# Index tiles turned by transposing transfers instead of TensorE, and the low parts of the looked-up weights and of the paired stage's h made on GpSimd

## The reference

```python
# attention, on the normalised x; scores are 512 x 512 per batch
q, k, v = x @ Wq, x @ Wk, x @ Wv
attn_scores = jnp.einsum('bes,bfs->bef', qT, kT) / np.sqrt(HEAD_DIM)
attn_weights = jax.nn.softmax(attn_scores, axis=-1)
attn_output = jnp.einsum('bef,bfs->bes', attn_weights, vT)
return jnp.einsum('bse,ef->bsf', jnp.swapaxes(attn_output, 1, 2), Wo)
...
# feed-forward network: w = lut[idx], three index matrices of 1376 x 512 int32 (down is 512 x 1376)
gate = _ghost_linear(x, gate_idx, lut)
up = _ghost_linear(x, up_idx, lut)
h = jax.nn.silu(gate) * up
return _ghost_linear(h, down_idx, lut)
...
x = x + attn(layernorm(x)); x = x + ffn(layernorm(x))
```

## Time and profile before

| | |
|---|---|
| Median of 3 runs | 1046.42 us (1044.93 to 1046.98) |
| The profiled execution's own time | 1046.57 us |
| Its span, first to last instruction | 1044.6 us |
| PE busy | 1010.1 us, 97% of the span |
| DVE, ACT, POOL busy | 485.5, 465.3, 134.5 us |
| DVE busy in the 40 slices of 26 us | 5 to 9 tenths up to slice 15, then 0 to 4 |

### The profile page before, as it was taken

One profiled execution on the slowest core, in us unless ns is written; L12 is line 12 of the kernel. 1 busy time (PEld: TensorE's weight loads), 2 busy tenths in 40 slices (PEclk: granted clock), 3 DMA queues, 4 the chain that ended last, 5 costly groups with the idle time before them and its releaser, 6 DMA issues.

```text
span 1044.6 us, 12958 instructions
## 1 busy us (share of the span) xinstructions
PE 1010.1 (97%) x4744; PEld 833.8 (80%) x4744; DVE 485.5 (46%) x1019; ACT 465.3 (45%) x753; POOL 134.5 (13%) x136
## 2 busy tenths in 40 slices
PE   5979999999999999999999999999999999999998
PEld 4878877878788868888888887888888888888886
DVE  5897998989999942311131113111311131112001
ACT  5999998797899921221222122212221222122111
POOL 5410000000000000110111011101110111011111
PEclk9999999999999999999999999999999999999999
DMA  9963012031011182200220002002200020001001
GB/s 239 200 170 103 21 54 89 6 129 46 29 71 49 66 317 86 101 1 1 81 81 1 1 1 82 1 1 81 81 1 1 1 81 1 1 1 41 1 1 40
DMA packets 31756, 61.42 MB, mean 59 GB/s; under 512 B 8704, under 2 KB 19152, under 8 KB 27344
## 3 DMA queue, kind: packets, MB, share of 16 engines
q1 hardware_dynamic: 18432, 54.40, 14.2%
q0 software_dynamic: 8944, 4.24, 3.5%
q10 hardware_dynamic: 4320, 1.97, 0.7%
HBM read 43.98 MB, written 20.84 MB: 62 GB/s over the span
## 4 chain that ended last, share of the span: by engine, by line
PE 80%; DVE 9%; ACT 5%; issue 3%; DMA 1%; POOL 1%; ACTq 0%; POOLq 0%; SPq 0%; DVEq 0%
PE bank L1018 44%; PE bank L1026 21%; PE bank L960 10%; DVE part L1208 2%; PE bank L1061 2%; DVE bn L1185 1%; PE bank L974 1%; DVE picked L1208 1%; PE bank L1007 1%; ACT part L753 1%; ACT xg_n L854 1%; ACT idx_out L846 1%; DVE xg_lo L1227 1%; DMA xg<-in_L_attn_x 1%; POOL rstd L717 1%
## 5 line engine op out<-in xcount | busy, mean ns | idle before, releaser
L1018 PE MATMUL bank<-x2t_hi,w_hi 128*128 128x512 f32 (+1 forms) x704 | 275.2, 391 | 3.8 <-DVE x2t_lo L1305 3.5
L1018 PE MATMUL bank<-x2t_hi,w_lo 128*128 128x512 f32 (+1 forms) x704 | 274.8, 390 | 0.0
L1018 PE MATMUL bank<-x2t_lo,w_hi 128*128 128x512 f32 (+1 forms) x704 | 274.7, 390 | 0.0
L1432 DVE TENSOR_TENSOR h_full<-bank,h_gate 128x512 f32<-128x512 f32 (+1 forms) x66 | 45.6, 691 | 396.5 <-PE bank L1018 396.5
L753 ACT ACTIVATE part<-high_bit,lut,lut_step 128x512 f32<-128x512 uint8 x198 | 154.5, 812 | 14.2 <-DVE part L1208 8.6
L1018 PEld LDWEIGHTS bank<-x2t_hi,w_hi 128*128 128x128 f32 (+1 forms) x704 | 130.8, 186 | 34.0 <-issue 4.7
L1018 PEld LDWEIGHTS bank<-x2t_lo,w_hi 128*128 128x128 f32 (+1 forms) x704 | 130.9, 186 | 29.6
L1018 PEld LDWEIGHTS bank<-x2t_hi,w_lo 128*128 128x128 f32 (+1 forms) x704 | 130.8, 186 | 29.2
L933 ACT ACTIVATE h_gate<-bank 128x512 f32<-128x512 f32 (+1 forms) x66 | 39.5, 598 | 256.5 <-PE bank L1018 256.5
L712 POOL TENSOR_TENSOR h_lo<-h_full,h_hi 128x512 fp32r<-128x512 f32 (+1 forms) x66 | 85.3, 1292 | 507.9 <-ACT h_hi L936 507.9
L1026 PE MATMUL bank<-w_hi,h_hi 128*128 128x512 f32 (+1 forms) x324 | 129.6, 400 | 0.1
(11 more groups left out here) (151 smaller groups left out, 1329.9 us busy)
## 6 DMA issues: line engine op xcount, KB each, us to landing
xg<-in_L_attn_x SPq DMA_DIRECT2D x7, 1024.0 KB, 6.8
x1a<-in_L_attn_x SPq DMA_DIRECT2D x4, 1024.0 KB, 4.9
out_dram<-x1a SPq DMA_DIRECT2D x4, 1024.0 KB, 3.9
x1b<-in_L_attn_x SPq DMA_DIRECT2D x3, 1024.0 KB, 4.9
m_hi<-m_scratch SPq DMA_DIRECT2D x3, 1024.0 KB, 4.8
m_lo<-m_scratch SPq DMA_DIRECT2D x3, 1024.0 KB, 6.9
out_dram<-x1b SPq DMA_DIRECT2D x3, 1024.0 KB, 3.9
h_scratch<-h_kept_hi SPq DMA_DIRECT2D x10, 256.0 KB, 2.0
```

The lines of the kernel that those rows point to most:

```text
L1018: last = pe.matmul(tile[0:n, :], a, x, start=(k == 0 and j == 0), stop=(k == K - 1 and j == 2))
L1432: dve.tensor_tensor(h_full[0:n, :], bank[5][0:n, :], h_gate[0:n, :], ALU.mult).then_inc(h_done, 1)
```

## The change

- PE's transposes of the index tiles, their PSUM copies on ACT and SP's stores of them are gone. In their place POOL's queue first casts the indices to uint16 from DRAM to DRAM (`narrow`, 19 transfers in six parts), SP issues 33 transposing transfers from there into eight SBUF buffers `idx_wide` (`turn_idx`), and POOL's queue stores each of these as bytes (`store_idx`).
- `narrow_at`, `turn_at` and `store_at` give the places: place i is Gram item i up to 31, and for entry `n` of the product stage it is n + 28. Turns 0 to 11 stand at places 9 to 30, turns 12 to 32 at places 31 to 51, one each; every store stands two places behind its turn.
- `weight_low` of all 33 tiles and `h_low` of the 22 pairs move from DVE to POOL (`weights_low`, with a table of its own, `POOL_LOOKS`).
- x of the Gram stage has four buffers instead of three (`idx_bf` is gone), so loads run a group further ahead.
- The tables are new. Their digits add up to this before the first product (`n` = 8): DVE 48 of 429 steps before, 21 of 396 now; ACT 33 of 294 before, 15 of 294 now; POOL 2 of 33 now. A tile has 13 steps on DVE before and 12 now.

```diff
+    NARROW = [slice(0, 1), slice(1, 2), slice(2, 4), slice(4, 6), slice(6, 8), slice(8, C)]
...
-        xg = [at(f"xg{i}", kib, [P, T, D], F32) for i, kib in enumerate((76, 84, 156))]
+        xg = [at(f"xg{i}", kib, [P, T, D], F32) for i, kib in enumerate((76, 84, 156, 92))]
...
-        idx_bf = [at(f"idx_bf{i}", 92 + 1 * i, [P, D], BF16) for i in range(16)]
-        idx_out = [at(f"idx_out{i}", 176 + i / 2, [P, D], U8) for i in range(4)]
+        idx_wide = [at(f"idx_wide{i}", 172 + i, [P, D], U16) for i in range(8)]
...
+        narrow_at = [2, 10, 16, 24, 30, 34]
+        turn_at = [9, 10, 11, 16, 18, 20, 22, 24, 26, 28, 29, 30] + list(range(31, 52))
+        store_at = [place + 2 for place in turn_at]
...
-            "0040000620100004200000062000004500010000600010009020000020202001007001008030000000902000801000601000"
-            "000000500000a04000d020060500402000d020080300702000c020060400602000c020080200802000c020070200401"
...
+            "0040050050000250000003300000053000004100010000800100007000000030003001008000009000300100823000700000"
+            "600002000000400000c00000e0000a0000700000c0000a0000900000d000090000800000g000070000800000e000080000e"
...
         @blk.sync
         def _(sp):
-            def store_idx(u):
-                if u < STRAIGHT:
-                    return
-                sp.wait_ge(idx_laid, u + 1)
-                sp.dma_start(idx_dram[u], idx_out[u % 4][:]).then_inc(idx_stored[u % 4], 16)
+            def turn_idx(u):
+
+                c, kind, slot = u // 3, u % 3, u % len(idx_wide)
+                if kind == 0:
+                    for part_, run in enumerate(NARROW):
+                        if run.start == c:
+                            sp.wait_ge(idx_narrowed[part_], 16 * (4 if run.stop == C else 3))
+                if u >= len(idx_wide):
+                    sp.wait_ge(idx_stored[slot], times_stored(u - len(idx_wide)))
+                n = rows(c)
+                if kind < 2:
+                    src = (gate_dram, up_dram)[kind][c * P:c * P + n, :]
+                    dst = idx_wide[slot][:].rearrange("p (k o) -> p k o", k=K)[:, :, 0:n]
+                else:
+                    src, dst = down_dram[:, c * P:(c + 1) * P], idx_wide[slot][:]
+                sp.dma_start(dst, src, transpose=True).then_inc(idx_turned[slot], 16)
...
-                if g >= 3:
-                    sp.wait_ge(xg_normed, T * (g - 2))
-                sp.dma_start(xg[g % 3][:], xb_dram[g]).then_inc(xg_loaded[g % 3], 16)
+                if g >= 4:
+                    sp.wait_ge(xg_normed, T * (g - 3))
+                sp.dma_start(xg[g % 4][:], xb_dram[g]).then_inc(xg_loaded[g % 4], 16)
...
+            def narrow(part_):
+
+                run, done = NARROW[part_], idx_narrowed[part_]
+                span = slice(run.start * P, min(run.stop * P, I))
+                for src, dst in ((gate_in, gate_dram), (up_in, up_dram)):
+                    pool.dma_start(dst[span, :], src[span, :]).then_inc(done, 16)
+                pool.dma_start(down_dram[:, span], down_in[:, span]).then_inc(done, 16)
+                if run.stop == C:
+                    pool.dma_start(down_dram[:, I:C * P], down_in[:, 0:C * P - I]).then_inc(done, 16)
+
+            def store_idx(u):
+
+                slot = u % len(idx_wide)
+                pool.wait_ge(idx_turned[slot], times_stored(u))
+                dst = idx_in[u][:] if u < STRAIGHT else idx_dram[u]
+                pool.dma_start(dst, idx_wide[slot][:]).then_inc(idx_stored[slot], 16)
...
-            for stage, arg in timeline:
-                if stage == "idx_load":
-                    load_idx(arg)
+            def weights_low():
+
+                for u in range(U):
+                    c, kind = u // 3, u % 3
+                    pool.wait_ge(w_hi_done, u + 1)
+                    low(w_lo[c][:, kind, :], picked[u % 2][:], w_hi[c][:, kind, :]).then_inc(w_lo_done, 1)
+                    yield
+
+            for stage, arg in with_looks(POOL_LOOKS, weights_low()):
+                if stage == "narrow":
+                    narrow(arg)
+                if stage == "idx":
+                    store_idx(arg)
...
+                if stage == "h_low":
+                    b, c = arg
+                    n, q = rows(c), pair_count[arg]
+                    hi, lo = h_kept if b else (h_hi[c % 2], h_lo[c % 2])
+                    pool.wait_ge(h_hi_done, q)
+                    low(lo[0:n, :], h_full[0:n, :], hi[0:n, :]).then_inc(h_lo_done, 1)
```

More of the change, by code:

```diff
@@ L162, in preln_attention_ghost_ffn @@
         xg_first_loaded = [sem(f"xg_first_loaded{t}") for t in range(T)]
-        xg_loaded = [sem(f"xg_loaded{i}") for i in range(3)]
+        xg_loaded = [sem(f"xg_loaded{i}") for i in range(len(xg))]
         xg_stats = sem("xg_stats")
@@ L315, in preln_attention_ghost_ffn @@
         timeline += [("gram_low", 0), ("stats_shift", 1), ("gram_n", 1), ("gram_in", 1), ("gram_n", 2), ("lut_step", 0)]
-        timeline += [("idx_load", u) for u in range(IDX_AHEAD)]
-        u = 0
         for i in range(T * NG):
@@ L333, in preln_attention_ghost_ffn @@
                 timeline.append(("gram_in", i + AHEAD))
[L334 to L336 removed]
+            index_steps(i)
             timeline.append(("gram", i))
@@ L684, in _ @@
             pool.memset(ident[:], 0.0).then_inc(const_made, 1)
-            pool.memset(ident_bf[:], 0.0).then_inc(const_made, 1)
-            for tile in idx_out:
-                pool.memset(tile[:], 0).then_inc(idx_cleared, 1)
-            pool.wait_ge(const_made, 2)
-            for one in (ident, ident_bf):
-                pool.affine_select(out=one[:], in_=one[:], compare_op=ALU.not_equal, fill=1.0, base=0,
-                                   pattern=[[-1, P]], channel_multiplier=1).then_inc(const_made, 1)
+            pool.wait_ge(const_made, 1)
@@ L1418, in _ @@
                     dve.tensor_tensor(h_full[0:n, :], pair_bank(arg)[1][0:n, :], h_gate[0:n, :], ALU.mult).then_inc(h_done, 1)
-                if stage == "h_low":
-                    b, c = arg
-                    n, q = rows(c), pair_count[arg]
-                    hi, lo = h_kept if b else (h_hi[c % 2], h_lo[c % 2])
-                    dve.wait_ge(h_hi_done, q)
-                    low(lo[0:n, :], h_full[0:n, :], hi[0:n, :]).then_inc(h_lo_done, 1)
             def ffn(b):
```

154 lines of the change are left out of this document (50 added, 104 removed).

## The result

The changed kernel takes **1051.89 us** (median of 6 runs, 1050.55 to 1055.12) against 1045.01 us of the kernel before (6 runs, 1043.39 to 1046.98) on the same chip: ratio **1.0068**, 95% interval 1.0055 to 1.008. It is slower by 7 us; 1031 was predicted. The profiled execution has a span of 1050.6 us.

What follows compares the result with a forecast made beforehand. PE was taken as the bound, with ACT full in the Gram stage and DVE close behind PE later. 1046.57 us less 17.7 (Gram) plus 2.2 (DVE beside POOL) gave 1031 us, range 1024 to 1057.

Steps and rivals of the forecast that it cites:

- The Gram stage: From Gram item 2 to the first product: 62.0 us in place of 79.7, a gain of 17.7 us.
- Later start and removed subtractions: DVE's work from first product to 372 us: 31.2 us removed, 10.6 added by later look-up, giving 238.4 us.
- The port's cost: POOL's subtractions beside DVE in product and paired stages: 0.57 us of DVE time each, 30.2 us for 53.
- The hold doesn't last for POOL's whole instruction: On the SBUF port: each POOL subtraction holds DVE only for its element-dependent part, 0.71 of 1.29 us.
- needs no second SBUF input: DVE's time outside copies and index operations, a fifth, was taken as spared from POOL's reads: factor 0.8.
- the idle term: DVE from first product on: half its present idle time, 7.3 us, stays as waits, so it needs 275.9 us.
- break-even of 0.86: DVE's cost per POOL subtraction, in us, at which the Gram stage's gain is eaten.
- more than 10 us in sum: Sign of failure after the Gram stage: PE's waits for low parts from POOL or DVE exceed this sum.
- the port held for whole instructions: Rival, chance 0.22: POOL's subtractions block DVE throughout, 54.7 us, so the kernel ends slower, at 1056 us.
- The free port: Rival, chance 0.15: POOL's reads slip between DVE's and cost nothing; 1026 us.
- The turns were not slow: Concerns a rival, chance 0.13: transposing transfers above 2.6 us each hold x1a and Wo; 1049 us at 3.5 each.
- the Gram stage keeps its gaps: Rival, chance 0.12: POOL's stores make rstd late or casts delay x; gain shrinks by 10 us, to 1041.

Runs made afterwards that it cites:

- e7: Changed kernel with all low parts on DVE and the look-up order of the kernel before, save steps the later indices forbid: 1049.8 us.
- e12: Changed kernel with all low parts on DVE, weight tiles 0 to 4 at its look-up places, exactly the old order from tile 5 on: 1040.8 us.
- e4: Kernel before, turning and look-up order kept, with only the low parts of weights and h moved to POOL: 1063.3 us.
- e5: Changed kernel with POOL writing zeros twice over each low part instead of subtracting, so without its reads; same queue, places and waits: 1035.6 us.
- e6: Kernel before, nothing moved, with POOL doing subtractions that nobody waits for at 52 places: 1070.9 us.
- e17: Changed kernel with stores of turned tiles 9 and later 14 entries further back in POOL's program alone: 1051.7 us.
- e9: Changed kernel with all low parts on DVE, weight tiles 0 to 6 at its look-up places, the rest at the old ones: 1044.0 us.
- e11: As e9, but with the 22 low parts of h on POOL: 1051.6 us.
- e8: As e7, but with all low parts on POOL as in the changed kernel: 1075.2 us.

## Why the prediction was wrong

- **The Gram stage** was right in its sum: 61.0 us from item 2 on, forecast 62.0, gain 18.7 for 17.7. ACT is busy 51.6 us, below the 55 named. Of the two reasons that the prediction gave, less work on PE and ACT from the transposes and fewer look-up steps, the first alone gained nothing in e7's order; the gain hung on the second.
- **Later start and removed subtractions** were right as loads. DVE's 273.8 us less the 35 of stretching are 238.8, and 238.4 was forecast.
- **The port's cost** was right in size, 0.65 us for 0.57, by luck, for both its parts were wrong. "The hold doesn't last for POOL's whole instruction": the copy of 304.59 waited for nearly all of POOL's. And the fifth of DVE's time that was left out since it "needs no second SBUF input" was not spared: the leaves alone took 12 of the 35 us, while the bit masks paid nothing (217 ns for 222). Why the mean comes out near half an instruction is not shown. DVE's load was 273.8 us, 268.6 forecast; that is 5.2 us of the miss.
- **The step that failed** is the idle term, "half of its present idle time", 7.3 us. Idle were 24.6, 17.3 us more, and 5.2 + 17.3 - 1.0 (Gram) is the 21.5 us by which the look-ups ended later (378.0) than by my sum (80.6 + 275.9 = 356.5). I took DVE as one full queue whose waits shrink. They did not shrink even without POOL: in e12, with all low parts on DVE, they are 20.7 us over both stages for 19.9 before; halved idle gives 1046.6 - 17.7 + 10.6 - 7.4 = 1032.1 us, whole idle 1039.5, and it took 1040.8. With POOL they grow. DVE and ACT feed each other in a fixed order, and now POOL stands in the same chain: a stretched copy delays a leaf, the leaf a cast, the cast a low part. e4 shows the growth without the turned path, from 19.9 to 31.6 us with DVE's load near the same; e5, in the changed kernel's own order, shows the waits between ACT and DVE shrink as the reads go. In e4 a piece costs 0.6 + 15.2 / 52 = 0.89 us on the path. The prediction's break-even of 0.86 counted on the halved idle time; with idle left whole it is 0.6 + (17.7 - 10.6) / 52 = 0.74. PE's waits for w_lo, 10.8 us, are the sign that the prediction had named for this step, "more than 10 us in sum".
- **Rivals.** The nearest in time was the port held for whole instructions, 1056 for 1052. It had the lock right and the change slower, and its 0.22 was too little, since the evidence against it was one copy beside a four-element power. But its number is near by luck: it put DVE's load at 293.1 us and idle at 7.3, and they were 273.8 and 24.6. The free port fell with e6; and e5, whose reads are gone, took 1035.6 us, not 1026. The turns were not slow: mostly 1.2 us each on SP. That the Gram stage keeps its gaps fell at once.
- **Left open**: what PE's lower granted clock after gaps adds (PE is busy 272.9 us for 266.1 with as many matmuls, so up to 6.8 us), and how near to the best any of the orders is. Differences of 10 us between assignments can be order; it was held only between e4 or e6 and the kernel before, e5 or e17 and the changed kernel, e9 and e11, and nearly so between e7 and e8.

## What to carry to other kernels

Before moving an elementwise operation with SBUF inputs from a nearly full DVE to GpSimd, price what DVE's other instructions lose beside it; here a subtraction of 0.6 us came back as 0.65 us of stretching, and as waits besides. When two engines feed each other in a fixed order, leave the idle time of before in the sum; here it stayed whole when work was moved within DVE, and grew when a third engine joined the chain. And a gain in one stage is real only when the work that ran beside it has another place; here the look-up moved behind the Gram stage took two thirds of its gain back.
